# A transformer block on one core: VectorE's row maxima and decode steps reordered, idle products added on TensorE, and the first half's attention output stacked in two column halves

## The reference

```python
h = _layernorm(x) * (1 + ca) + sa
# attention on h
c  = (h @ W_to_kv.T) @ W_compress.T            # 1024 x 32
ch = layernorm(c) * ln_gamma + ln_beta
q, k, v = ch @ W_q_comp.T, *split(ch @ W_kv_comp.T)
q, k = rope(q), rope(k)
o = softmax(where(causal, q k^T / sqrt(32), -1e30)) @ v
z = o @ W_comp2lat.T
x = x + ga * (z @ W_to_kv + z @ W_out_res.T + b_out_res)
h = _layernorm(x) * (1 + cb) + sb
gate, up = h @ Wg.T, h @ Wu.T                  # Wg, Wu, Wd decoded from 4-bit codes times scales
x = x + gb * ((gelu(gate) * up) @ Wd.T)
```

## Time and profile before

| | |
|---|---|
| median of 3 runs | 223.62 us (221.26 to 226.83) |
| profiled execution: device time | 223.54 us |
| profiled execution: span of the trace | 221.7 us |
| mean granted clock | 0.938 |
| PE busy | 198.0 us (89%) |
| DVE busy | 128.7 us (58%) |
| ACT busy | 98.2 us (44%) |
| POOL busy | 69.6 us (31%) |

### The profile page before, as it was taken

One profiled execution on the slowest core, in us unless ns is written; L12 is line 12 of the kernel. 1 busy time (PEld: TensorE's weight loads), 2 busy tenths in 40 slices (PEclk: granted clock), 3 DMA queues, 4 the chain that ended last, 5 costly groups with the idle time before them and its releaser, 6 DMA issues. The chain is left out here.

```text
span 221.7 us, 3054 instructions
## 1 busy us (share of the span) xinstructions
PE 198.0 (89%) x1041; PEld 161.4 (73%) x1041; DVE 128.7 (58%) x238; ACT 98.2 (44%) x161; POOL 69.6 (31%) x64
## 2 busy tenths in 40 slices
PE   7899988979658599998979799999899999999991
PEld 2798658547436268787867698898588888888891
DVE  0547575839583538898979886633933233233234
ACT  2213435536331868446262447644252543543420
POOL 4326932490150356000021000441615615615200
PEclk9956996969958799999999999999999999999999
DMA  6999665200000000000000000000020000000002
GB/s 207 351 298 261 207 216 188 97 0 3 0 0 0 1 0 3 0 0 1 3 0 0 0 0 3 1 0 1 13 85 1 0 0 0 0 0 0 3 0 95
DMA packets 4765, 11.31 MB, mean 51 GB/s; under 512 B 560, under 2 KB 1744, under 8 KB 4624
## 3 DMA queue, kind: packets, MB, share of 16 engines
q1 hardware_dynamic: 4336, 10.82, 15.5%
q10 hardware_dynamic: 416, 0.33, 0.5%
HBM read 10.09 MB, written 1.05 MB: 50 GB/s over the span
## 5 line engine op out<-in xcount | busy, mean ns | idle before, releaser
L928 PE MATMUL ps<-H,WS 128*128 128x512 f32 x384 | 95.9, 398 | 6.0 <-ACT wmod_flat L459 4.0
L928 PEld LDWEIGHTS ps<-H,WS 128*128 128x128 f32 x384 | 70.8, 191 | 22.1 <-ACT wmod_flat L459 5.0
L928 PEld LDWEIGHTS ps<-WS,IS 128*128 128x128 f32 x384 | 49.8, 191 | 3.2 <-issue 0.6
L928 PE MATMUL ps<-WS,IS 128*128 128x256 f32 x384 | 51.3, 283 | 0.4 <-DVE wmod_flat L781 0.2
L465 ACT ACTIVATE IS<-wmod_flat 128x512 fp32r<-128x512 f32 x32 | 20.2, 633 | 59.1 <-PE ps L928 33.1
L771 DVE TENSOR_TENSOR wmod_flat<-ps,wmod_flat 128x512 f32<-128x512 f32 x32 | 22.1, 689 | 29.6 <-PE ps L928 18.5
L299 DVE TENSOR_TENSOR IS<-wmod_flat,IS 128x512 fp32r<-128x512 f32 x32 | 22.3, 697 | 26.4 <-ACT IS L465 25.7
L308 POOL TENSOR_TENSOR WS<-wbuf,WS 128x1024 fp32r<-128x1024 f32 x10 | 23.9, 2389 | 36.6 <-ACT WS L444 36.6
L313 POOL TENSOR_TENSOR WS<-wbuf,WS 128x512 fp32r<-128x512 f32 x10 | 13.3, 1327 | 42.5 <-ACT WS L453 42.3
L459 ACT ACTIVATE wmod_flat<-ps 128x512 f32<-128x512 f32 x32 | 18.8, 586 | 5.9 <-PE ps L928 5.8
L547 POOL TENSOR_TENSOR rstd<-var,power 128x4 f32<-128x4 f32 x6 | 8.2, 1371 | 40.7 <-DVE var L629 33.5
(11 more groups left out here) (124 smaller groups left out, 218.6 us busy)
## 6 DMA issues: line engine op xcount, KB each, us to landing
wbuf<-packed SPq DMA_DIRECT2D x8, 384.0 KB, 17.4
wbuf<-scales SPq DMA_DIRECT2D x8, 384.0 KB
wmod_flat<-wmod SPq DMA_DIRECT2D x1, 1024.0 KB, 9.8
out<-head SPq DMA_DIRECT2D x4, 256.0 KB, 2.2
head<-x SPq DMA_DIRECT2D x1, 576.0 KB, 3.9
wmod_flat<-wmod SPq DMA_DIRECT2D x1, 512.0 KB, 5.6
head<-x SPq DMA_DIRECT2D x1, 512.0 KB, 7.4
rope_sb<-rope SPq DMA_DIRECT2D x2, 256.0 KB, 11.6
```

What stands on the lines that cost most here:

```text
L928: return pe.matmul(o, lhsT, rhs, start=start, stop=stop)
```

## The change

Five kinds of edit, in the diff below:

- The decode steps before unit n go from 2 n to 2 n + 2, at least 8 (`STEPS_AT_START`), so eight instead of four of them stand before and between the blocks of half 1's attention, and all later ones one unit earlier. The number of steps is the same.
- VectorE's program where half 1's attention meets units 0 and 1: `split_v(1)` and one decode step of group 1 move up ahead of `stage_h0`, and both parts of `row_max(1)` move up ahead of `inter_full(1)` and `inter_low(1)`. GpSimd's `add_bias(1)` moves from behind its four `probs_low` to ahead of them.
- ScalarE computes one exponential of a 2-column tile, whose result is not used, behind `split_d(1, 1)`; so the exponential's table is loaded there and not at half 1's first exponential.
- Half 0's fourth block of key scores gets a bank of its own (4), so all four blocks of key scores are issued in a row before the first `attend`.
- Half 0's output is rounded and stacked in two halves of 256 columns, its `output` waits for each half apart, and its sums are inverted in pairs. ScalarE rounds both halves before VectorE starts on the first.
- `stay_warm` is called at eight more places, and with more products at two old ones. In the program's order it adds 3, 2, 2, 1, 2, 1, 3, 1, 2 and 4 products, 21 in all, to the 19 of before.

The diff, without the reordering that the tables above show:

```diff
-STEPS_AT_START = 4
+STEPS_AT_START = 8
...
+        def key_bank(h, b):
+
+            return b if h == 0 and b < 3 else 4 if h == 0 else 4 + b % 3
+
+        def o_parts(h):
+
+            return ((0, HALF),) if h else ((0, HALF // 2), (HALF // 2, HALF))
...
             def out_high(h):
                 act.wait_ge(pv_done, all_blocks(h))
                 if h == 1:
-                    act.wait_ge(o_ready, 1)
-                act.activation(o_hi[:], bank(4 * h + 3), ACT.Copy).then_inc(o_hi_ready, 1)
+                    act.wait_ge(o_ready, 2)
+                for c0, c1 in o_parts(h):
+                    act.activation(o_hi[:, c0:c1], ps[:, 4 * h + 3, c0:c1], ACT.Copy).then_inc(o_hi_ready, 1)
...
+            split_d(1, 1)
+            act.activation(silu_t[:, 1, :], silu_t[:, 0, :], ACT.Exp)
             spread(3)
             max_rows(1)
...
+            add_bias(1)
             for b in range(1, 2 * HT, 2):
                 probs_low(pool, 1, b, b + 1)
-            add_bias(1)
...
             def out_stack(h):
...
+                for q, (c0, c1) in enumerate(o_parts(h)):
+                    dve.wait_ge(o_hi_ready, 3 if h else 2)
...
+                    dve.scalar_tensor_tensor(OS[:, c0:c1], o_hi[:, c0:c1].bitcast(F32), cst[:, C_OM:C_OM + 1],
+                                             ps[:, 4 * h + 3, c0:c1], ALU.mult, ALU.add).then_inc(o_ready, 1)
...
             def steps_before(n):
 
-                return STEPS_AT_START + 2 * (n - 2)
+                return max(STEPS_AT_START, 2 * n + 2)
...
             rotate(1)
+            split_v(1)
...
             norm2(0, (0, 1))
+            decode(1, 1, 2)
             stage_h0()
...
             for b in range(0, 2 * HT, 2):
-                decode_more(min(4, 1 + b // 2), min(4, 2 + b // 2))
+                decode_more(b, b + 2)
                 probs_low(dve, 1, b, b + 1)
...
             def output(h):
-                pe.wait_ge(o_ready, h + 1)
                 pe.wait_ge(wo_ready, 1)
                 for j in range(HT):
+                    pe.wait_ge(o_ready, 3 if h else j // 2 + 1)
...
             transpose1(0)
+            stay_warm(WC_B, 3)
...
             mod_columns(bank(CA_B, KT), CA, False).then_inc(moda_done, 1)
+            stay_warm(5, 2)
...
             mod_columns(bank(SA_B, KT), SA, False).then_inc(moda_done, 1)
+            stay_warm(5, 2)
             project_c(0, 0, HT)
...
             project_qkv(0)
+            stay_warm(5, 1)
             stack_qk(0)
             project_c(1, 2, HT)
+            stay_warm(5, 2)
             scores(0, 0, HT)
             max_rows(0)
-            stay_warm(0, 2)
-            key_scores(0, 0, 0)
-            key_scores(0, 1, 1)
-            key_scores(0, 2, 2)
+            stay_warm(0, 3)
+            for b, k in blocks(0):
+                key_scores(0, b, k)
...
+            stay_warm(5, 3)
             attend(0, 0, 0)
-            key_scores(0, 3, 3)
+            stay_warm(5, 1)
             attend(0, 1, 1)
...
             transpose_c(1)
+            stay_warm(5, 2)
             output(0)
...
             project_qkv(1)
-            stay_warm(7, 4)
+            stay_warm(7, 8)
             stack_qk(1)
```

More of the change, by code:

```diff
@@ L492, in _ @@
             qk_high(1)
-            for n in range(2):
-                gelu(n, n, False)
-                inter_hi(n, n, False)
-                (split_gu, split_d)[n](1, 1)
+            gelu(0, 0, False)
+            inter_hi(0, 0, False)
+            split_gu(1, 1)
+            gelu(1, 1, False)
+            inter_hi(1, 1, False)
+            split_d(1, 1)
+            act.activation(silu_t[:, 1, :], silu_t[:, 0, :], ACT.Exp)
             spread(3)
@@ L692, in out_stack, with softmax_sums @@
             def out_stack(h):
-                dve.wait_ge(o_hi_ready, h + 1)
-                if h == 1:
-                    dve.wait_ge(ao_done, HT)
-                dve.scalar_tensor_tensor(OS[:], o_hi[:].bitcast(F32), cst[:, C_OM:C_OM + 1], bank(4 * h + 3),
-                                         ALU.mult, ALU.add).then_inc(o_ready, 1)
-            def softmax_sums(h):
-                dve.wait_ge(ao_done, HT * (h + 1))
-                link(dve.reciprocal(rden[:, HT * h:HT * (h + 1)], ps[:, 4 * h:4 * h + HT, D]))
+                for q, (c0, c1) in enumerate(o_parts(h)):
+                    dve.wait_ge(o_hi_ready, 3 if h else 2)
+                    if h == 1:
+                        dve.wait_ge(ao_done, HT)
+                    dve.scalar_tensor_tensor(OS[:, c0:c1], o_hi[:, c0:c1].bitcast(F32), cst[:, C_OM:C_OM + 1],
+                                             ps[:, 4 * h + 3, c0:c1], ALU.mult, ALU.add).then_inc(o_ready, 1)
+            def softmax_sums(h, first, end):
+                dve.wait_ge(ao_done, HT * h + end)
+                link(dve.reciprocal(rden[:, HT * h + first:HT * h + end], ps[:, 4 * h + first:4 * h + end, D]))
             def residual1(h, j):
@@ L842, in _ @@
             out_stack(0)
-            softmax_sums(0)
+            softmax_sums(0, 0, 2)
             residual1(0, 0)
@@ L846, in _ @@
                 if i < HT - 1:
+                    if i == 1:
+                        softmax_sums(0, 2, HT)
                     residual1(0, i + 1)
@@ L855, in _ @@
             norm2(0, (0, 1))
+            decode(1, 1, 2)
             stage_h0()
-            split_v(1)
             split_qk(1)
-            decode(1, 1, 3)
+            decode(1, 2, 3)
             inter_full(0, 0, False)
+            decode(1, 3)
             inter_low(dve, 0, 0, False)
-            decode(1, 3)
+            row_max(1, 0, HT)
             inter_full(1, 1, False)
+            row_max(1, HT, len(pieces(1)))
             inter_low(dve, 1, 1, False)
-            row_max(1, 0, HT)
-            decode_more(0, 1)
-            row_max(1, HT, len(pieces(1)))
             for b in range(0, 2 * HT, 2):
-                decode_more(min(4, 1 + b // 2), min(4, 2 + b // 2))
+                decode_more(b, b + 2)
                 probs_low(dve, 1, b, b + 1)
@@ L881, in _ @@
                 elif n == 3:
-                    softmax_sums(1)
+                    softmax_sums(1, 0, HT)
                 elif n in (4, 6):
@@ L1053, in key_scores @@
                 pe.wait_ge(ones_ready, 7)
-                if b >= 3:
+                if b >= 3 and h:
                     pe.wait_ge(p_full, k - 2)
@@ L1057, in key_scores @@
                 diag = b >= HT * h
-                last = mm(ps[:, 4 * h + b % 3, c0:HALF], KS[:, P * b:P * (b + 1)], QS[:, h, c0:], True, not diag)
+                last = mm(ps[:, key_bank(h, b), c0:HALF], KS[:, P * b:P * (b + 1)], QS[:, h, c0:], True, not diag)
                 if diag:
-                    last = mm(ps[:, 4 * h + b % 3, c0:c0 + P], identb[:], maskb[:, 1, :], False, True)
+                    last = mm(ps[:, key_bank(h, b), c0:c0 + P], identb[:], maskb[:, 1, :], False, True)
                 last.then_inc(st_done, 1)
```

2 lines of the change are left out of this document (1 added, 1 removed).

## The result

The changed kernel takes 211.31 us (median of four runs, 209.06 to 213.57) against 223.64 us; the ratio is 0.945, with a 95% interval of 0.931 to 0.959. Run again later it gave 210.46 us and a ratio of 0.948 (0.940 to 0.957). The forecast was 211.8 us, with a range of 206.0 to 218.0. Its profiled execution took 212.09 us with a span of 210.3 us, 11.4 us less than the span before.

The account below looks back on a forecast made before the run. TensorE is busy nearly throughout from 84 us; winnable time lay in its low clock before 50 us and its waits for maxima, remainders and `gelu`. The terms sum to -11.7, so 223.5 becomes 211.8 us, range 206.0 to 218.0.

Parts of the forecast that it names:

- maxima first: Between units 0 and 1, VectorE's earlier row maxima bring half 1's first key scores forward: -6.8 us (bounds -7.2 and -4.4).
- table forward: Before half 1's first exponential, the 1.28 us table load moves into ScalarE's wait for `max_rows(1)`: -1.3 us.
- decode steps in the blocks: In half 1's blocks, more decode steps line up with VectorE's and GpSimd's remainders: +2.8 us (bounds -1.7 and +4.5).
- decode earlier in the MLP: Between 84 and 130 us, decoding one unit earlier cuts TensorE's waits for `gelu`: -2.5 us (bounds -4.0 and -0.5).
- idle before `stack_qk(1)`: Eight idle products fill the gap before `stack_qk(1)`, which then runs at the high clock: -1.3 us (bounds -1.5 and +0.2).
- early idle products: From 10.4 to 20.6 us, seven idle products win half of the gain from a high clock: -1.6 us.
- half 0's scores and blocks: In half 0's attention, 3.4 us at the low clock go: -0.9 us (bounds -1.4 and +0.6).
- output in halves: At half 0's output, the wait before the reciprocal goes, a second reciprocal is added: -0.1 us (bounds -0.6 and +0.3).
- the first: Rival, chance 0.22: half 1's blocks aren't bound by VectorE and GpSimd together; -1.2 instead of +2.8, giving 207.8 us.
- The second: Rival, chance 0.15: idle products leave the clock as it was; +0.2, +1.5, +0.6 instead of -3.8 together, giving 217.9 us.
- the third: Rival, chance 0.03: the 21 idle products lie on the path at the low clock; +10.9, giving 226.5 us.
- the fourth: Rival, chance 0.15: VectorE's backlog, not the decode's date, makes the MLP's waits; -0.5 instead of -2.5, giving 213.8 us.

Follow-up runs that it names:

- e3: The kernel before with only VectorE's reordering around the row maxima between units 0 and 1: 219.35 us, ratio 0.973.
- e4: The changed kernel without the exponential that loads the table ahead: 210.86 us, ratio 0.936.
- e10: e8 without the exponential that loads the table ahead: 212.34 us, ratio 0.950.
- e2: The changed kernel with the decode steps placed as in the kernel before: 213.51 us, ratio 0.951.
- e11: The kernel before with only the 21 added idle products: 223.32 us, ratio 0.991.
- e8: The changed kernel with two decode steps moved behind half 1's blocks, six instead of eight before their end: 210.40 us, ratio 0.950.
- e1: The changed kernel with the 19 idle products of the kernel before instead of 40: 213.84 us, ratio 0.951.
- e7: The changed kernel without the seven early idle products before `project_c(0)`: 211.31 us, ratio 0.950.
- e5: The changed kernel with six decode steps between half 1's blocks replaced by products of two SBUF tensors: first exponential to `gate_up(3)` 12.66 us.
- e6: As e5, but one input of each replacement product is read from PSUM: first exponential to `gate_up(3)` 12.30 us.

## Why the prediction was right, term by term

Term by term, from the two traces that it was made for (before and changed):

| term | predicted | measured | |
|---|---|---|---|
| maxima first | -6.8 | -6.8 | e3: -7.4 by itself; 0.57 lost in `gate_up(0)` |
| table forward | -1.3 | -0.7 | e4, e10: 0.72 |
| decode steps in the blocks | +2.8 | +2.6 | e2, e3, e11: about +1.1; 1.2 is clock |
| decode earlier in the MLP | -2.5 | -4.2 | e2: 3.8 of waits; e8: by the date, not the load |
| idle before `stack_qk(1)` | -1.3 | -1.5 | e1, e3, e11 |
| early idle products | -1.6 | +0.6 | e7: clock not held |
| half 0's scores and blocks | -0.9 | -1.3 | e1, e3, e11: the fall at 34 us is gone by the idle products |
| output in halves | -0.1 | 0.0 | |
| sum | -11.7 | -11.3 | span: -11.4 |

The middle was right in its mechanism, and in its size to the 0.57 us in `gate_up(0)` that no term had: the four maxima start at 54.9 instead of 62.84, the wait of 4.41 us is gone, and what is late next is `gate_up(2)` itself, as said. The output's two halves did what was said of them: the wait before the reciprocal shrank from 0.84 to 0.46 and not to nothing, and the second reciprocal took back the gain.

Four terms were mis-sized or matched in part by luck. The sum came out right because the MLP's 1.7 us too little and the early products' 2.2 us too much cancel:

- The MLP term. The step that failed was "VectorE was busy 40.9 of 46 us, and is 37.5 of 42 even then", from which I kept 1.5 of the 4.0 us of waits. The runs show that VectorE's load was not the reason: it was busy 39.46 of 44 us in e2, with 3.8 us of waits, and 41.81 in e8, with 0.8. The waits came from the date at which ScalarE finds a group decoded, and went completely with one unit of lead. The measured -4.2 lies outside the bounds of this term (-4.0 and -0.5).
- The early idle products. I took "half of the gain" where the rows gave no reason for any: the stretch consists of products of 1 and 32 columns, and seven idle products did not keep the clock up. The bad end of that term, the delay alone, was what happened (+0.6, where I had put +1.5 at most). One of the prediction's own signs failed with it: the clock was to be at 1.00 for part of 10 to 20 us, and was low from 10.9 to 21.2, for 10.2 us as before.
- The table. I priced the load by its own length and did not ask what the first exponential would wait for next: its key scores, 0.59 us. That is the rule that I had applied to the maxima a paragraph above.
- The blocks. The count of one-after-another time gave 15.3 us and 15.16 were measured, but the count has `down(1)` at 1.6 us, the high clock, and it took 2.80. In e4 it took 1.65 and the blocks 13.95. And e2, e3 and e11 show that the old order takes 12.5 to 14.2 us, by the clock. The mechanism holds (e5 against e6), but not all of the work was lined up; the agreement of the size is luck in part.

Of the rivals, the first (a looser overlap, 207.8 us, with the blocks 1.2 us shorter) is refuted: there are decode steps of 1.6 to 1.9 us, and the blocks got longer. It was right in so far as the overlap is looser than the count. The second is true for the early products and false for those in half 0's blocks and before `stack_qk(1)`; the third needed 16 of 21 idle products on the path, and e1 and e11 show that all together they gain; the fourth, that VectorE's backlog makes the MLP's waits, is refuted by e2 and e8.

## What to carry to other kernels

Where a slow engine waits for another, look at what that other engine does just ahead of the awaited instruction, and move the awaited one up: such a reordering on VectorE was worth 5.8 us of 225 by itself, and it kept TensorE's clock high in the stretch behind it without idle products (though not in the blocks that followed). Producing an operand a full unit early removed all of TensorE's waits from a pipelined stretch in which VectorE was about 90% busy, so a high busy share is no reason to expect that waits stay. Before a ratio is called better than another, look at what the base took beside each of them. When a stall is taken away, price it by what is late next, not by its own length.
